# The second token half's operands: made in slices during the first half and kept in DRAM

## What is computed

```python
def _L0_attn_ref(hidden_states, wq, wkv, wo):
    H = 32
    DN = 128
    DR = 64
    DV = 128
    HID = 512
...
    q = jnp.einsum('bsd,de->bse', hidden_states, wq).reshape(B, S, H, DQ)
    kv = jnp.einsum('bsd,de->bse', hidden_states, wkv)
...
    scores = jnp.einsum('bqhd,bkhd->bhqk', q[..., :DN], k) * scale
...
    probs = jax.nn.softmax(scores, axis=-1)
    attn = jnp.einsum('bhqk,bkhd->bqhd', probs, v).reshape(B, S, H * DV)
    return jnp.einsum('bse,ed->bsd', attn, wo)
```

## Time and profile before

| what | value |
|---|---|
| median of 3 runs (lowest to highest) | 2157.1 us (2154.85 to 2158.34) |
| the profiled execution: its own time | 2158.86 us |
| its span in the trace | 2157.1 us |
| TensorE busy | 2108.3 us, 98% |
| VectorE / GpSimd / ScalarE busy | 62% / 58% / 34% |
| mean granted TensorE clock | 0.991 |

### The profile page before, as it was taken

The page is one execution under the profiler, slowest core; times in us unless marked ns, Lnnn a source line. Parts: engine busy times, 40 slices in busy tenths (PEclk is TensorE's granted clock), DMA queues, the critical chain, the costliest instruction groups (busy, mean ns, idle before and its releaser), DMA issues. The chain is left out here.

```text
span 2157.1 us, 36235 instructions
## 1 busy us (share of the span) xinstructions
PE 2108.3 (98%) x11876; PEld 1822.5 (84%) x11876; DVE 1338.5 (62%) x2465; ACT 730.9 (34%) x1454; POOL 1255.8 (58%) x1315
## 2 busy tenths in 40 slices
PE   7899999999999998999999999999999999999999
PEld 5788888989888897889898898989887777778887
DVE  7656565665656567665666566566666666654444
ACT  5233232332323233332323233232333645443332
POOL 3587585766758575767758576775844732114220
PEclk9999999999999999999999999999999999999999
DMA  7411112111111210311111211111112200001110
GB/s 238 149 50 40 40 42 65 49 39 39 39 39 40 66 50 30 88 40 40 39 39 39 68 49 39 39 39 39 40 61 78 92 14 0 0 0 40 39 39 19
DMA packets 92036, 107.57 MB, mean 50 GB/s; under 512 B 5569, under 2 KB 71777, under 8 KB 90817
## 3 DMA queue, kind: packets, MB, share of 16 engines
q1 hardware_dynamic: 90689, 102.53, 15.7%
q0 software_dynamic: 1280, 4.20, 0.7%
HBM read 100.79 MB, written 5.94 MB: 49 GB/s over the span
## 5 line engine op out<-in xcount | busy, mean ns | idle before, releaser
L215 PE MATMUL psum<-yc,wh 128*128 128x512 f32 x904 | 363.4, 402 | 9.5 <-DVE yc L1499 5.0
L216 PE MATMUL psum<-yc,wh 128*128 128x512 f32 x904 | 354.6, 392 | 0.0
L217 PE MATMUL psum<-yc,wh 128*128 128x512 f32 x904 | 354.2, 392 | 0.0
L1359 DVE TENSOR_TENSOR resid<-psum,resid 128x512 f32<-128x512 f32 x248 | 171.3, 691 | 148.5 <-PE psum L217 144.3
L215 PE MATMUL psum<-kept,yc 128*128 128x256 f32 x896 | 255.9, 286 | 1.7 <-DVE v_tok L1309 1.0
L941 POOL TENSOR_TENSOR wh<-wh_f,wh 128x256 fp32r<-128x256 f32 x256 | 191.8, 760 | 110.9 <-ACT wh L907 109.0
L217 PE MATMUL psum<-kept,yc 128*128 128x256 f32 x896 | 253.5, 283 | 0.0
L216 PE MATMUL psum<-kept,yc 128*128 128x256 f32 x896 | 253.4, 283 | 0.0
L215 PEld LDWEIGHTS psum<-yc,wh 128*128 128x128 f32 x904 | 171.6, 190 | 43.3 <-DVE yc L1499 5.8
L217 PEld LDWEIGHTS psum<-yc,wh 128*128 128x128 f32 x904 | 170.9, 189 | 36.6
L941 POOL TENSOR_TENSOR wh<-raw,wh 128x256 fp32r<-128x256 f32 x192 | 142.2, 741 | 96.2 <-ACT wh L907 96.2
(11 more groups left out here) (355 smaller groups left out, 4818.5 us busy)
## 6 DMA issues: line engine op xcount, KB each, us to landing
raw<-in_attn_w SPq DMA_DIRECT2D x96, 512.0 KB, 4.8
wo_f<-in_attn_w SPq DMA_DIRECT2D x31, 512.0 KB, 4.0
hankel<-kernel_rows SPq DMA_DIRECT2D x32, 256.0 KB, 4.7
resid<-in_xT SPq DMA_DIRECT2D x4, 1024.0 KB, 9.8
outT<-wide SPq DMA_DIRECT2D x16, 256.0 KB, 2.6
kept_f<-in_l_w SPq DMA_DIRECT2D x3, 1024.0 KB, 5.5
work_f<-in_oct_w SPq DMA_DIRECT2D x4, 680.0 KB, 4.1
resid<-in_xT SPq DMA_DIRECT2D x4, 512.0 KB, 6.1
```

The source lines that it names most:

```text
L215: pe.matmul(out, w[0], x[0], start=start, stop=False)
L216: pe.matmul(out, w[0], x[1], start=False, stop=False)
L217: return pe.matmul(out, w[1], x[0], start=False, stop=stop)
L1359: dve.tensor_tensor(part, psum[:, 5 + (GH + m) % 3, :], part, ALU.add).then_inc(tail_free, 1)
```

## The change

`yc` of the second pass is no longer made between quads 7 and 8. In each of quads 0 to 7, VectorE makes an eighth of each of the seven combinations: 64 of the 512 token columns (`part_of_y`), in the order j = 0, 4, 3, 1, 2, 5, 6, at seven places of the quad. Each part is two to five operations on 128 partitions x 128 elements in a small buffer `stage` (high and low part), and there is one `stage`. ScalarE issues a DMA that stores it to a DRAM tensor `y_parts` in runs of 256 bytes (`store_part`), and VectorE waits for the landing of one part (`part_out`) before it begins the next. Over the eight quads these are 56 stores of 128 KB, and VectorE has 21 more operations in a quad. In quad 7 SyncE loads `yc` from `y_parts`, 1 MB for each j (`load_y`), as soon as TensorE is done with product j of quad 7's last set; TensorE in quad 8 waits for these landings (`y_in`). The separate orders of quads 7 and 8 are gone: they are those of any other quad. The loads of `x` wait only until all parts are made.

```diff
+        PART_ORDER = (0, 4, 3, 1, 2, 5, 6)
+        PART_STEPS = [2 + n for n in (0, 1, 0, 2, 1, 3, 0)]
...
+            def load_y(it, j):
+                sp.wait_ge(prod_done, product_count(it * SETS + SETS - 1, j))
+                sp.wait_ge(part_out, 16 * (it * 7 + PART_ORDER.index(j) + 1))
+                if j >= 2:
+                    sp.wait_ge(y_in[j % 2], 16 * (j // 2))
+                sp.dma_start(yc[:, j].bitcast(F32), y_parts[j]).then_inc(y_in[j % 2], 16)
+
             def body(it, pair, first=False, turn=False, turned=False, last=False):
                 q = it - pair * QUADS
                 hw.load_values(sp, t, it, q)
                 if turned:
-                    sp.wait_ge(y_ready, 7)
+                    sp.wait_ge(part_step, parts_done(QUADS, 0))
...
+                    if turn:
+                        for j in range(7):
+                            load_y(it, j)
...
         def _(act):
-            def combination_high(pair, js):
...
+            def store_part(it, j):
+                wait_apart(act, part_step, parts_done(it, PART_ORDER.index(j) + 1), hw.passed)
+                act.dma_start(y_parts[j][:, :, :, slice_of(it)], stage[:].bitcast(F32)).then_inc(part_out, 16)
...
+                store(4)
 
                 keep_p5(it, 3)
                 out_high(it * 2 + 1)
+                store(3)
                 keep_p1(it, 4)
...
+            def part_of_y(it, j):
+
+                def block(k, m):
+                    return resid[:, 2 * k:2 * k + 2, bass.ds(it * (TT // QUADS) + (HALFTOK + m * TT), TT // QUADS)]
+
+                b11, b12, b21, b22 = (block(k, m) for k in range(2) for m in range(2))
+                raw, n = stage_raw[:, 1], PART_ORDER.index(j)
+                done = parts_done(it, n)
+                if n or not (isinstance(it, int) and it == 0):
+                    wait_apart(dve, part_out, it * 112 + 16 * n, hw.passed)
+                terms = {1: ((b12, b11, ALU.subtract), (b22, raw, ALU.subtract)), 2: ((b12, b11, ALU.subtract),),
+                         4: ((b22, b12, ALU.subtract),),
+                         5: ((b21, b11, ALU.subtract), (raw, b22, ALU.subtract), (raw, b12, ALU.add))}.get(j, ())
...
+                dve.tensor_copy(stage[:, 0], source).then_inc(part_step, 1)
+                dve.wait_ge(part_step, done + (n + 1))
+                dve.tensor_tensor(stage[:, 1], source, stage[:, 0].bitcast(F32), ALU.subtract).then_inc(part_step, 1)
...
                 elif fresh == 1:
-                    pe.wait_ge(y_ready, j + 1)
+                    pe.wait_ge(y_in[j % 2], 16 * (j // 2 + 1))
```

More of the change, by code:

```diff
@@ L1031, in quads, with slice_of, parts_done @@
             body(2 * QUADS - 1, 1, last=True)
[L1033 to L1037, removed]
+        def slice_of(it):
+            return bass.ds(it * (TT // QUADS), TT // QUADS)
+        def parts_done(it, n):
+            return it * sum(PART_STEPS) + sum(PART_STEPS[:n])
         def half(i):
@@ L1189, in body, with store @@
             def body(it, pair, first=False, turn=False, turned=False, last=False):
+                def store(j):
+                    if pair == 0:
+                        store_part(it, j)
                 hw.high(act, it, "H1", (0,))
+                store(0)
                 keep_p5(it, 0, first)
-                if turned:
-                    combination_high(1, (5, 6))
-                if not first and not turned:
+                if not first:
                     exps(it * 4)
@@ L1228, in body @@
                 o_high(it * 4 + 2)
+                store(1)
                 hw.high(act, it, "H3", (1, 2, 3))
@@ L1231, in body @@
                 hw.high(act, it, "H3", (4, 5, 6))
+                store(2)
                 o_high(it * 4 + 3)
-                if turn:
-                    combination_high(1, (0,))
+                store(5)
                 if not last:
@@ L1238, in body @@
                 keep_p5(it, 5)
[L1239 to L1242, removed]
+                exps(it * 4 + 3)
                 if last:
-                    act.wait_ge(c2_in, 16)
+                    act.wait_ge(x1_c2_in, 16 * (KC + 1))
                     for i in range(4):
@@ L1250, in body @@
                     hw.high(act, it + 1, "H0", (1, 2, 3))
+                    store(6)
                     keep_p1(it + 1, 0)
                     hw.high(act, it + 1, "H0", (4, 5, 6))
-                    if turn:
-                        exps(it * 4 + 3)
             act.sem_inc(exp_done, 1)
@@ L1272, in _ @@
         def _(dve):
[L1273 to L1284, removed]
@@ L1363, in body, with part @@
                 sm, T = it * 4, it * 4
+                def part(j):
+                    if pair == 0:
+                        part_of_y(it, j)
                 mix(it, 0, 0)
[L1366 to L1370, removed]
+                part(0)
+                if not first:
                     soft_shift(sm)
                 mix(it, 0, 1)
-                if turned:
-                    combination_low(1, 6)
-                elif not first:
+                if not first:
                     soft_divide(sm)
                 mix(it, 0, 2)
-                if turned:
-                    soft_shift(sm)
-                elif not first:
+                if not first:
                     soft_turn(sm, 1, it * 8)
                 mix(it, 0, 3)
-                if turned:
-                    soft_divide(sm)
                 mix(it, 0, 4)
-                if turned:
-                    soft_turn(sm, 1, it * 8)
                 mix(it, 1, 0)
@@ L1424, in body @@
                 mix(it, 2, 4)
+                part(4)
                 mix(it, 3, 0)
@@ L1428, in body @@
                 mix(it, 3, 1)
+                part(3)
                 mix(it, 3, 2)
@@ L1433, in body @@
                 mix(it, 4, 0)
+                part(1)
                 o_low(T + 2)
```

79 lines of the change are left out of this document (30 added, 49 removed).

## The result

The changed kernel takes 2146.8 us (median of 5 runs, 2144.9 to 2148.2), the kernel before 2157.1 beside it: ratio 0.9948, 95% interval 0.9937 to 0.9959. It is faster, by 10.3 us. The forecast was 2143, the range 2140 to 2153. The profiled execution took 2145.5 us.

What follows compares the result with a forecast made beforehand. TensorE alone bounds ordinary quads, so only the turn could gain: 2158.86 - 14.63, plus 0.8 for places read as free, gives 2145.0 profiled; the median, 1.76 lower, is forecast at 2143 us, range 2140 to 2153.

Steps and rivals of the forecast that it cites:

- The turn: Window from quad 7's to quad 8's second scores: becomes like quad 6, 14.63 us less, waits and slow matmuls together.
- place one: Set 3, quads 0 to 7: part 3 waits for part 4's store; landing 3 to 4.5 us, 5.5 free, no cost.
- rival A: Store at set 3 takes 5.5 to 7 us, or set 4's over 3.8: 2 to 12 us lost, some 2150; chance 0.15.
- Place two: End of set 4: part 5 waits for part 2's store; landing up to 3.8 us is free, cost nothing.
- VectorE's load: Quads 0 to 7: 21 added operations, 5.7 us per quad, plus one GpSimd hold-up of about 1.0; covered by slack.
- The `yc` loads: Loads from quad 7 to quad 8: worst takes 7.4 us of 10.0 available, so cost nothing.
- The sum: Whole kernel: 2158.86 - 14.63 + 0.8 gives 2145.0 profiled; median 1.76 below, so 2143 us.
- B: At the turn, `yc` loads are late: a 2 us wait and slow matmuls give back half, 2150; chance 0.09.
- C: At set 3, the store lands with the last of the loads: 16 us lost against 14.6, 2158; chance 0.07.
- D: As C, but TensorE's clock falls behind each 2 us wait: 25 us lost, 2168; chance 0.06.

Runs made afterwards that it cites:

- two buffers: Against the changed kernel: from quad 1 on, parts alternate between `stage` and a used-up slice of `resid`, a semaphore each; 2143.6 us, ratio 0.9937.
- two put back: Against the changed kernel: parts 4, 3 and 2 stand right behind the `mix` on P7, beside GpSimd's; parts 0 and 1 unmoved; 2142.2 us, ratio 0.9924.

## Why the prediction was right, and where it was off

**The turn: right.** 14.63 us were to go, 14.3 did, and the slow matmuls went with the waits. The missing 0.3 is place one in quad 7.

**Place one: the mechanism right, the landing mis-sized.** The step "I take a value of 3 to 4.5 us (the quiet 2.6 and a share of the traffic), since the store has a sixteenth of those loads' 2 MB, so no cost" failed. It landed after 4.8 to 5.4 us, and the free time was 4.8, not 5.5: the store is issued 0.23 us after part 4 is done, part 3 starts 0.24 us after the landing, and the `mix` needs a little more ahead of P3. The cost was 0.04 to 0.6 us in each of quads 1 to 6, 2.2 in all, and 0.3 in quad 7, where the sum had 0.1 per quad. The quads of the first pass got longer than those of the second (94.52 to 94.57), which the prediction had named as the sign of a late landing. Quad 0's 0.4 us is another term: part 4's own operations ahead of a `mix`, which the prediction had at nothing. This is rival A at its low end, by its loss per quad; its landing of 5.5 us or more wasn't reached. The rule of the Trainium skill that I had weighed beside it (DMA: Bandwidth & Descriptors, section Queues, rings and completion order: round-robin by packet between rows) would have made the store free. It was not, and with a quarter of the pieces it landed no sooner.

**Place two: right.** Part 2's store lands in 2.3 us; no matmul waits there.

**VectorE's load: too low.** The prediction had 5.7 us per quad and one hold-up of 1.0; it is 8.4, since parts 1 and 6 lie beside GpSimd. In the changed kernel these places have the slack, as the kernel with two buffers shows (94.54 with parts 1 and 6 in place). But I had priced a hold-up from one row and no rival asked what it costs elsewhere. The same parts in other places lose 18 us, more than the turn gives.

**The `yc` loads: right.** The worst took 7.4 us, as estimated, and no matmul waited.

**The sum.** For the profiled execution it had 2145.0; that took 2145.5. The quads lost 1.8 us more than allowed, and the part of the program behind quad 15's second scores was 1.4 us shorter. Its windows, before and after:

```profile
1529.76:2157.09 627.33, 610.15 (x3079) 502.35 (x3077) 369.20 (x702) 255.85 (x470) 212.07 (x207) 0.99 0.11 34
1517.72:2143.68 625.96, 607.93 (x3079) 500.55 (x3077) 370.34 (x702) 255.75 (x470) 212.28 (x207) 0.99 0.11 34
```

The same 3079 matmuls are busy for 2.2 us less. Over the twelve traces, in which nothing differs there, this part takes 625.0 to 627.6 us, and 627.6 is that of a kernel with the change in it (two put back). The five longest (626.6 to 627.6) are the five with the lowest granted clock there, 0.986 to 0.989. So the 1.4 us lie within what this part varies from execution to execution, and are not shown to be a gain of the change. The remaining miss of the median (2146.8 against 2143) is mostly its conversion: I took the median 1.76 below the profiled execution, and here it is 1.3 above. The 0.63 that I gave to 2141 to 2145.5 missed; 2146.8 lies in rival A's stretch.

**The rivals.** A happened in small. B, C and D did not happen. Forced, C costs 19 us, near the 16 computed, but 6.6 of them in quad 0 and 1.6 to 2.0 in each other quad; D's slow matmuls did not come behind waits of up to 1.7 us. Against D the prediction had set that the slow rows of before stand behind a wait of 3.9 us. It overlooked the wait of 2.8, some 4 us after the clock had come back to 1.00, behind which the matmuls come every 0.43 us instead of 0.23 (PE, before):

```profile
860.53 0.77 PE L215 MATMUL psum<-yc,wh 128*128 128x512 f32 x1 [2.76 <-DVE qk L1309]
861.10 0.63 PE L216 MATMUL psum<-yc,wh 128*128 128x512 f32 x1
861.52 0.63 PE L217 MATMUL psum<-yc,wh 128*128 128x512 f32 x1
```

So D was nearer than it looked, and between 1.7 and 2.8 us it stays open.

## What to carry to other kernels

When an engine's step waits for a DMA landing, look at what is queued behind it on that engine: moving one `mix` ahead of the wait gave the loss of quads 1 to 7 back, with the landing as late as ever. Price a store's landing from the rows of its neighbours in time, not from a quiet one: under 2 MB of loads it took twice as long. Put short VectorE operations with two SBUF inputs, and casts, where GpSimd is idle, or where nothing on the critical path is behind them; the same 21 operations cost 0 or 18 us by place.

Two edits each bring quads 1 to 6 to 94.5 us: part 3 behind the `mix` on P7 (2142.8 us, ratio 0.9936), or parts 4 and 3 a set earlier and part 2 earlier in set 4 (2142.2, 0.9924). Their intervals overlap the change's, so the medians alone don't show their lead; the windows show 2.2 us of it in quads 1 to 6 and 0.2 at the turn, and the second edit 0.35 in quad 0.

## What the runs showed of the hardware

- VectorE operations of 0.29 us (two SBUF inputs) and 0.23 us (cast) took 1.2 to 2.39 us beside GpSimd ones of 1.29 to 2.40, to 0.1 to 0.15 us behind GpSimd's end; GpSimd's took in the mean at most 0.06 us longer than before. In the changed kernel two `mix`es, with an input in PSUM, kept their 0.69 us beside GpSimd's 2.39 us one.
- TensorE came back at the pace of 1.2 GHz behind waits of 2.76, 3.56, 3.92 and 4.39 us, and at full pace behind waits of 1.0 and 1.7 us.
- A store of 128 KB landed in 2.3 us in the quiet (1.9 in pieces of 1 KB) and in 4.8 to 5.6 us beside four loads of 512 KB, in pieces of 256 bytes or of 1 KB alike (with two buffers 4.6 to 6.3). Issued 1.5 us after a single such load, it took 4.3.
